# Second normalisation of a two-layer graph network: fp16 halves transposed and multiplied with halves of the score weights, eight tiles in the block ahead, the gap between the layers reordered

## What is computed

```python
# layer 0
h = maximum(layernorm(x), 0)
A = (adj != 0); deg = A.sum(axis=0)
x = x + (A @ (h @ W0 + b0)) / deg[:, None]
# layer 1: attention with 4 heads
h = maximum(layernorm(x), 0)
ht = (h @ W1) split into 4 heads of 512
src, dst = ht @ a_src, ht @ a_dst              # one number for each row and head
e = leaky_relu(src[:, None] + dst[None, :], 0.01) + adj
x = x + mean over heads of softmax(e) @ ht
```

## Time and profile before

| | us |
|---|---|
| median of three timed runs (2478.62 to 2480.04) | 2478.82 |
| the profiled execution, its own time | 2480.18 |
| its span, from the first to the last instruction | 2478.1 |
| TensorE busy in the span | 2454.2 |
| the gap, from PE's first step of the last block (L1508) to its first matmul of layer 1 (L824) | 348.99 to 444.82 |

### The profile page before, as it was taken

The page is one execution under the profiler, slowest core; times in us unless marked ns, Lnnn a source line. Parts: engine busy times, 40 slices in busy tenths (PEclk is TensorE's granted clock), DMA queues, the critical chain, the costliest instruction groups (busy, mean ns, idle before and its releaser), DMA issues.

```text
span 2478.1 us, 42814 instructions
## 1 busy us (share of the span) xinstructions
PE 2454.2 (99%) x12358; PEld 1200.9 (48%) x12358; DVE 1873.2 (76%) x2575; ACT 1260.7 (51%) x1886; POOL 47.8 (2%) x44
## 2 busy tenths in 40 slices
PE   7999999999999999999999999999999999999999
PEld 4444446444444444444444444444444444444787
DVE  7788767976688776887768777687766887667776
ACT  5645645744455444554445544455445554444554
POOL 0000000000000000000000000000000000000000
PEclk9999999999999999999999999999999999999999
DMA  4375746100131001310013100131000300001000
GB/s 149 105 267 186 250 153 220 59 4 5 35 89 34 4 4 34 89 35 4 4 34 89 35 4 4 33 90 35 4 4 26 97 34 3 3 13 49 26 1 9
DMA packets 74079, 143.95 MB, mean 58 GB/s; under 512 B 4473, under 2 KB 11899, under 8 KB 72826
## 3 DMA queue, kind: packets, MB, share of 16 engines
q1 hardware_dynamic: 73978, 142.82, 18.1%
HBM read 129.11 MB, written 13.70 MB: 58 GB/s over the span
## 4 chain that ended last, share of the span: by engine, by line
PE 95%; DVE 2%; DMA 1%; issue 1%; ACT 0%; SPq 0%; DVEq 0%; ACTq 0%
PE z_ps L768 71%; PE o_ps L796 11%; PE o_ps L1455 3%; PE z_ps L1455 3%; PE z_ps L1508 2%; PE o_ps L1420 1%; PE c_ps L1420 1%; DMA ring_reg<-adjT_in 1%; PE c_ps L1455 1%; PE c_ps L1487 1%; DVE hl_reg L969 1%; PE o_ps L1405 1%; PE o_ps L1479 0%; DVE w_reg L1004 0%; PE c_ps L782 0%
## 5 line engine op out<-in xcount | busy, mean ns | idle before, releaser
L768 PE MATMUL z_ps<-hl_reg,h_reg 128*128 (+2 forms) x8712 | 1751.8, 364 | 1.3 <-DVE hl_reg L629 1.3
L768 PEld LDWEIGHTS z_ps<-hl_reg,h_reg 128*128 (+1 forms) x8712 | 852.5, 98 | 897.3 <-issue 1.8
L570 ACT ACTIVATE hl_reg<-t_reg (+2 forms) x363 | 360.7, 994 | 723.3 <-DVE t_reg L657 379.6
L629 DVE TENSOR_TENSOR hl_reg<-t_reg,hl_reg (+2 forms) x363 | 416.5, 1147 | 229.5 <-ACT hl_reg L570 227.1
L555 ACT ACTIVATE t_reg<-ring_reg,vv 128x512 f32 (+3 forms) x728 | 526.4, 770 | 66.2 <-DVE ao_reg L644 60.8
L657 DVE SCALAR_TENSOR_TENSOR t_reg<-t_reg,vv,e_reg (+3 forms) x728 | 510.6, 744 | 9.9 <-issue 7.9
L644 DVE TENSOR_TENSOR ao_reg<-ao_reg,t_reg 128x1024 f32<-128x1024 f32 (+1 forms) x336 | 384.0, 1143 | 0.0
L796 PE MATMUL o_ps<-w_reg,z_reg 128*128 128x512 f16 x1248 | 278.2, 379 | 0.9 <-DVE z_reg L673 0.9
L796 PEld LDWEIGHTS o_ps<-w_reg,z_reg 128*128 128x128 f16 x1248 | 119.8, 98 | 140.9 <-DVE z_reg L673 1.2
L673 DVE SCALAR_TENSOR_TENSOR z_reg<-z_ps,z_reg 128x512 f16<-128x512 f32 (+1 forms) x112 | 73.2, 653 | 151.6 <-ACT z_reg L582 151.6
L463 ACT ACTIVATE e_reg<-e_reg (+2 forms) x91 | 90.5, 995 | 152.5 <-DVE e_reg L474 152.5
(11 more groups left out here) (177 smaller groups left out, 1096.8 us busy)
## 6 DMA issues: line engine op xcount, KB each, us to landing
ring_reg<-adjT_in SPq DMA_DIRECT2D x78, 512.0 KB, 4.6
e_reg<-adjT_in SPq DMA_DIRECT2D x78, 512.0 KB, 3.7
ring_reg<-x_in SPq DMA_DIRECT2D x13, 512.0 KB, 4.1
x_dram<-ring_reg SPq DMA_DIRECT2D x13, 512.0 KB, 5.0
ao_reg<-x_dram SPq DMA_DIRECT2D x6, 1024.0 KB, 5.5
out_dram<-ao_reg SPq DMA_DIRECT2D x6, 1024.0 KB, 4.4
ring_reg<-c_dram SPq DMA_DIRECT2D x23, 256.0 KB, 3.4
h_reg<-x_in SPq DMA_DIRECT2D x3, 1536.0 KB, 16.5
```

The source lines that it names most:

```text
L570: nc.scalar.activation(hl_ring[:, g % HL_RING, 0, :, 0:W], t_ring[:, g % T_RING, :, 0:W], ACT.Copy).then_inc(hi_ready, 1)
L629: nc.vector.tensor_tensor(hl_ring[:, g % HL_RING, 1, :, 0:W], t_ring[:, g % T_RING, :, 0:W], hl_ring[:, g % HL_RING, 0, :, 0:W], ALU.subtr ...
L768: mm = nc.tensor.matmul(z_ps[:, k, 0:W], hk[hs], hl_ring[:, r, ps, u, 0:W], start=first and u == 0 and n == 0, stop=last and u == 1 and n ...
```

## The change

In five parts.

1. **Transposes and scores in fp16.** All tiles but the last one transpose their two fp16 halves, eight transposes of 128x128 fp16 instead of four of fp32; ACT copies 128x1024 fp16 out of PSUM instead of 128x512 fp32; the scores take eight matmuls with fp16 weights (the transposed halves) against 16 columns (high and low half of `wa`). A tile's transpose now waits for the DVE subtraction that makes the low half (`st1_split`), and no longer only for the normalised tile. `wa` is scaled and split in layer 0 by a few small DVE instructions; the two halves of the scores are added before their maximum (`sdc`).
2. **Eight tiles in the block ahead.** The sums and statistics of tiles 0 to 7 are made between steps 80 and 90 of layer 0's `awork` (`early1`), with x loaded into the stage (`load_early`), and tiles 0 to 3 are also normalised and split there. Tiles 4 to 7 follow at the gap's start.
3. **Order in the gap.** `LN1_AT` goes from ceil(6 + 5m/3) to ceil(5 + 1.9m), so that the last of these tiles comes after step 51 and not after step 46; `MR_AT` from 24 to 28. On DVE a pair's subtraction stands between the sums of the group after it. The reductions of the maximum stand behind the scalars of groups 2, 3 and 4 instead of 0, 1 and 2.
4. **The last block's halves.** The halves of tiles 20 to 22 go to a buffer of their own (`late_h`) and are copied into `h16` by a DMA when layer 0 is done with that space; the first loop of layer 1 on PE waits for it (`late_in`).
5. **The tail.** The first activation of layer 1 reads the spread row from PSUM and does not wait for its copy; `keep_clock` is 15, 2, 9 and 11 instead of 14, 0, 12 and 14; ACT's first exponentials, and DVE's first steps of layer 1, stand in another order.

```diff
@@ constants
-        LN1_AT = [math.ceil(6 + 5 * m / 3) for m in range(NT - 1)]
+        LN1_AT = [math.ceil(5 + 1.9 * m) for m in range(NT - 1)]
-        MR_AT = 24
+        MR_AT = 28
+        SUM_G = LAST0 + 2
@@ DVE, layer 0 and the gap
+                def early1(n):
+                    if n == 0:
+                        degrees1(0, EARLY)
+                        x1_sums(0, 2)
+                    if n == 1:
+                        x1_sums(2, 4)
+                    if n == 2:
+                        variances1(0)
+                        ln_scalars(dve, *groups1[0], NG0)
+                    if n == 4:
+                        split1(0)
+                        degrees1(EARLY, 2 * EARLY)
+                    if n == 5:
+                        split1(1)
+                    if n == 8:
+                        x1_sums(4, 6)
+                    if n == 9:
+                        x1_sums(6, 8)
+                    if n == 10:
+                        variances1(1)
+                        ln_scalars(dve, *groups1[1], NG0 + 1)
...
+                    early1(g - SUM_G)
+                degrees1(2 * EARLY, NT)
...
                     for i in range(i0, i1, 2):
-                        for k in range(i, min(i + 2, i1)):
-                            x1_tile(k)
-                        for k in range(i, min(i + 2, i1)):
-                            x1_stats(k)
-                    ln_variances(dve, t0, t1, x1_bst, i1, s_mv1, i1)
-                    while split < min(i0 // 2, LATE_SPLIT):
+                        x1_sums(i, min(i + 2, i1))
+                        if split < min(i0 // 2, PAIRS - 1):
+                            split1(split)
+                            split += 1
+                    variances1(c)
+                    while split < min(i0 // 2, PAIRS - 1):
                         split1(split)
                         split += 1
                     ln_scalars(dve, t0, t1, NG0 + c)
-                    if c < len(late_max):
-                        reduce_max(late_max[c], len(early_max) + c, o_ps[:, 2])
+                    if 0 <= c - 2 < len(late_max):
+                        reduce_max(late_max[c - 2], len(early_max) + c - 2, o_ps[:, 2])
@@ DVE, first steps of layer 1
-            for p in range(1, 4):
-                step(0, 0, p, before=(0, 0, p - 1) if p > 1 else None, lone=p == 1)
...
+            step(0, 0, 1, lone=True)
+            subtract_max(dve, 0, E_PRE0 + 2)
+            lo_part(0, 0, 1)
+            step(0, 0, 2, lone=True)
+            accumulate(0, 0, 1)
+            subtract_max(dve, 0, E_PRE0 + 3)
+            step(0, 0, 3)
+            split1_one(1)
@@ ACT, layer 0 and the gap
                 for g in range(NA):
+                    if g == SUM_G + 2:
+                        ln_sqrt(act, *groups1[0], NG0)
+                    if g == NA - 1:
+                        ln_sqrt(act, *groups1[1], NG0 + 1)
                     degrees(g)
+                    for j in range(2):
+                        if g == SUM_G + 3 + j:
+                            act.wait_ge(s_ln, NG0 + 1)
+                            relu1(2 * j)
+                            relu1(2 * j + 1)
+                            high1(j)
...
+                    if i < NT - 1:
+                        nc.scalar.activation(ht1_16[:, i % 2], o16[:, i % 2].rearrange("p (s k i) -> p s k i", s=2, k=KT),
+                                             ACT.Copy).then_inc(tr_sb, 1)
...
+                for c in range(2, 5):
+                    relus1(c)
+                    for j in (2 * c, 2 * c + 1):
+                        relu1(2 * j)
+                        transposed1(back)
+                        relu1(2 * j + 1)
+                        high1(j)
+                        if j == 2 * c + 1:
+                            next_sqrt(c)
+                        transposed1(back + 1)
+                        back += 2
...
-                for p in range(E_PRE0 - 1):
-                    exp_e(act, 0, p)
+                exp_e(act, 0, 0)
@@ PE
                 def transpose1(i):
-                    pe.wait_ge(st1_ready, i + 1)
...
+                    if i < NT - 1:
+                        pe.wait_ge(st1_split, unit(i) + 1)
+                        pe.wait_ge(s_i16, 1)
+                        h = late_h[:, t - L0] if L0 <= t < L0 + 3 else h16[:, t]
+                        for s in range(2):
+                            for k in range(KT):
+                                mm = nc.tensor.transpose(o16[:, i % 2, (s * KT + k) * P:(s * KT + k + 1) * P],
+                                                         h[:, s, k * P:(k + 1) * P], ident16)
...
                 scores(NT - 2)
                 pe.wait_ge(mr_sb, 1)
                 pe.wait_ge(st1_split, 1)
-                keep_clock(14)
+                keep_clock(15)
                 transpose1(NT - 1)
+                keep_clock(2)
                 scores(NT - 1)
-                keep_clock(12)
+                keep_clock(9)
```

More of the change, by code:

```diff
@@ L1286, in w1_high @@
                     act.wait_ge(wr_in[k], 16)
[L1287 removed]
+                    nc.scalar.activation(w16[:, k, :, 0], w_again, ACT.Copy, scale=wsc[:, 0:1]).then_inc(w_hi, 1)
                 def w0_high(k):
@@ new lines, in high1_one, with relus1, next_sqrt @@
+                    h = late_h[:, 2] if u == 0 else h16[:, tiles1[NT - 1]]
+                    nc.scalar.activation(h[:, 0], ln1_stage[:, (PAIRS - 1) % 2, u], ACT.Copy).then_inc(hi1_done, 1)
+                def relus1(c):
+                    act.wait_ge(s_ln, NG0 + c + 1)
+                def next_sqrt(c):
+                    ln_sqrt(act, *groups1[c + 1], NG0 + c + 1)
+                relus1(1)
+                relu1(4)
+                relu1(5)
+                high1(2)
+                transposed1(0)
@@ new lines, in _ @@
+                for c in (5, 6):
+                    i0 = tiles_of(c)
+                    relus1(c)
+                    relu1(i0)
+                    transposed1(back)
+                    relu1(i0 + 1)
+                    high1(i0 // 2)
+                    next_sqrt(c)
+                    transposed1(back + 1)
+                    back += 2
+                    if c == 5:
+                        max_rows()
+                transposed1(back)
+                relus1(7)
+                relu1(NT - 2)
@@ L1378, in _ @@
+                high1_one(0)
+                for i in range(back + 1, NT - 1):
+                    transposed1(i)
+                next_sqrt(7)
+                relus1(8)
+                relu1(NT - 1)
                 transposed1(NT - 1)
-                for p in range(E_PRE0 - 1):
-                    exp_e(act, 0, p)
+                exp_e(act, 0, 0)
                 act.wait_ge(s_dn, 1)
-                for q, f in ((0, 1.0), (1, SLOPE)):
-                    nc.scalar.activation(ev4[:, q], dn3, ACT.Exp, scale=f / HS).then_inc(s_vv, 1)
+                for q in range(2):
+                    nc.scalar.activation(ev4[:, q], dn3, ACT.Exp, scale=wacoef[:, q:q + 1]).then_inc(s_vv, 1)
@@ L1384, in _ @@
                 act.wait_ge(s_carg, 1)
-                nc.scalar.activation(cc3, cc3, ACT.Exp, scale=1.0 / HS).then_inc(s_cexp, 1)
-                exp_e(act, 0, E_PRE0 - 1)
-                act.wait_ge(cb_ps, 1)
-                act.wait_ge(x1_out[0], 16 * sum((NA + i) % ADJ_RING == 0 for i in range(PAIRS)))
-                nc.scalar.activation(c_bc[:, 0], o_ps[:, 1], ACT.Copy).then_inc(c0_sb, 1)
+                nc.scalar.activation(cc3, cc3, ACT.Exp, scale=wacoef[:, 0:1]).then_inc(s_cexp, 1)
@@ L1391, in c_rows, with c_first @@
+                exp_e(act, 0, 1)
+                def c_first():
+                    act.wait_ge(x1_out[0], 16 * sum((NA + i) % ADJ_RING == 0 for i in range(PAIRS - EARLY)))
+                    nc.scalar.activation(c_bc[:, 0], o_ps[:, 1], ACT.Copy).then_inc(c0_sb, 1)
                 def c_rows():
```

341 lines of the change are left out of this document (215 added, 126 removed).

## The result

| | before | after |
|---|---|---|
| median, us | 2479.33 (2476.95 to 2481.26, 20 runs) | 2482.74 (2480.03 to 2485.62, 20 runs) |
| ratio, 95% interval | | 1.0016 [1.001, 1.0022] |
| the profiled execution, its own time | 2480.18 | 2481.89 |
| its span | 2478.1 | 2480.2 |

The change made the kernel 3.4 us slower by the medians, 0.14 to 0.16%, so within the 0.2% that the prediction called no change (the interval reaches 0.22%). The two profiled executions are 1.7 us apart, their spans 2.1.

A forecast was written before the change was run, and what follows sets the result against it. PE was taken as the bound, busy 99% of the span. Last step 431.9 against 429.7, less 1.0 for the tail, gave +1.2 us on 2480.18, or 2480.0 against the median; range 2470 to 2487.

The forecast's parts named there:

- The tail: From layer 0's last step to layer 1's pairs on PE: -0.6 to -1.2 us, taken as -1.0.
- Both rivals on a slow PE: Gap: fp16 transposes (about 2485 us) or score weights (about 2486) at fp32 pace; 0.25 for either or more low clock.
- the rival with a copy of 0.48: ACT in the gap: copy takes 0.48 us, last step 423.7, or 426.9 with low clock, 2475 us; faster case's chance 0.28.
- the walk: Gap: PE, ACT and DVE queues stepped in order, instructions starting when engine and inputs are ready; last step 427.9 at full clock.
- first maximum: Gap's start: PE's step 4 waits 0.6 us for ACT's copies, standing behind group 1's square root.
- second maximum: Gap: PE waits 3.3 us, from 361.4, for DVE's reduction behind group 2's scalars.
- third maximum: Gap: PE waits 5.8 us, from 372.3, for DVE's reduction behind group 3's scalars.
- waits for copies up to the last step: PE waits for ACT copies behind square roots: 2.1 us at tile 10's scores, 0.3 at 15, 2.2 at 16, 1.8 at 18.
- low clock: PE at 1.2 GHz after long waits in the gap: moves the last step from 427.9 to 431.9 us.
- the sum of work and waits: Gap to the last step: PE's work ending at 411.8 us plus 16.1 of waits gives 427.9 at full clock.
- the ring: Block ahead, steps 80 to 90: it covers PE, so most of DVE's 19.7 us of waits is free for early work.
- PE alone: Gap: PE's work without waits, 62.8 us to step 51, would end at 411.8, 17.9 us earlier.

The follow-up runs named there:

- the experiment on the loads: Changed kernel with the two early loads of x (tiles 0 to 3) issued at step 80 of the adjacency's loads instead of 76: 2480.9 us, ratio 1.0009.
- the tail alone: Kernel before the change plus only its fifth part, without the extra fillers (9 and 11 instead of 12 and 14): 2478.48 us, ratio 0.9996.

## Why the prediction was right, and where a term was wrong

**PE's work fell as forecast.** Transposes 0.445 us a tile (0.44 said), scores 0.20 (0.25 said). The Trainium skill (TensorE: Matmul & The Clock Gate, "LDWEIGHTS (loading the stationary operand)") would have, by its formula, an estimated 107 ns for each of the scores' weight loads; the runs show 25 ns for load and matmul together, here and with the scores doubled. The same page ("Back-to-back issue gap") puts a sustained stream of loads and 128-column matmuls at about 81 ns each; the transposes are such a stream and run at 56. Both rivals on a slow PE fell with these rows.

**The copy on ACT** takes 0.91 us (0.96 said): elements count, not bytes. So the rival with a copy of 0.48 fell; the half-width copy shows that such a copy would be worth 4.6 us with the reductions repaired.

**The waits came where the walk put them.**

| | said | measured |
|---|---|---|
| first sums in the gap, us | 353.1 | 354.5 |
| first maximum, PE's wait | 0.6 (step 4) | 0.4 |
| second maximum | 3.3 | 2.97 |
| third maximum | 5.8 | 5.73 |
| waits for copies up to the last step | 2.1 + 0.3 + 2.2 + 1.8 = 6.4 | 1.92 + 2.01 + 1.59 = 5.5 |
| all waits up to the last step | 16.1 | 14.7 |
| low clock: said, what it adds net of later waits; measured, its own loss | +4.0 | +4.1 |
| the block, start to last step's end, against before | 82.9 - 80.7 = +2.2 | 82.1 - 80.7 = +1.4 |

That the waits for the maxima were the cause, and not only present, is shown twice (from DVE's side and from PE's): without them the kernel is 8 us faster than before. The clock's 4.1 is from that experiment, and close to what the windows give. That it matches the 4.0 said is in part luck. The prediction reckoned with five waits long enough for the low clock and settled near what its walk gave for four such stretches (431.6); for two it had 430.5, so +2.6. Two came: behind 2.97 and 5.73 us, and not behind 1.92, 2.01 and 1.59. But the second was twice as long (5.4 us at 0.50, 2.7 lost), and the measured 4.1 stands beside waits that are already 1.4 shorter than said. The 0.8 by which the block is shorter than said are the scores (23 tiles at 0.05, so 1.2) and the waits (1.4), less about 1.7 in short gaps of PE that the sum of work and waits doesn't hold; it missed 0.7 of such in the kernel before.

**What failed is this step:** "The loads and stores added to SP's queue are 512 KB each, 4.1 us to landing, and go out at least 6 us ahead of use, while DVE is throttled by the ring; I cost them at nothing." The loads were not late for their own use. They made the adjacency late, in a stretch (281 to 307 us) in which the ring doesn't throttle DVE and DVE has no idle time that could take it up. The term is 1.3 us at PE's restart and 1.6 at layer 1, by the experiment on the loads; the first sums in the gap moved with it (353.2 there, 354.5 in the changed kernel, 353.1 said). I had read the ring's cover at steps 80 to 90 in the earlier trace rows and applied it to loads that are issued four steps and more ahead of these.

**The tail** was said to give 1.0 and gives 0.86. These are its rows in the changed kernel:

```profile
434.36 3.40 PE L1730 MATMUL o_ps<-h_reg 128*128 128x512 f16 x15
437.60 0.60 PE L1664 MATMUL o_ps<-ident,z_reg 128*128 128x128 f32 x4
...
442.89 0.65 PE L1743 MATMUL o_ps<-ident,rows_c 128*128 128x128 f32 x4 [1.00 <-ACT rows_c L1557]
...
446.76 5.35 PE L853 MATMUL z_ps<-hl_reg,h_reg 128*128 128x512 f16 x24 [0.74 <-DVE hl_reg L764]
452.63 5.35 PE L797 MATMUL z_ps<-hl_reg,h_reg 128*128 x24 [0.52 <-DVE hl_reg L656]
458.74 3.62 PE L797 MATMUL z_ps<-hl_reg,h_reg 128*128 x16 [0.76 <-DVE hl_reg L656]
```

From the last step to the last tile's transposes 437.60 - 432.6 = 5.0 us against 4.2 (+0.8; +0.85 said). From there to the spread 5.29 against 6.53 in the earlier trace rows and the row that follows them at 440.43 (-1.24; -0.4 to -1.05 said). To the first pair 3.87 against 4.39 (-0.52; -0.6 said). From the first to the third pair 11.98 against 11.88 (+0.1; -0.4 said): the second pair's gain of 0.8 is given back whole at the third, as the tail alone showed too. Two misses of opposite sign.

**The sum.** +1.5 at the block's start, gap +1.4, tail -0.86: +2.0, and the spans differ by 2.1. Of the 1.5 the experiment gives 1.3 to the loads (the block starts at 349.17 there, at 348.99 before); 0.2 has no run of its own. The prediction's +1.2 was +2.2 - 1.0. Its miss is this 1.5 us, against 0.8 too much for the gap: the close total owes something to errors of opposite sign. By the medians the difference is 3.4; what the other 1.3 are is not shown: a profiled execution is one of many, and these spread over 5.6 us. The wait at 305 us, which varies from 1.0 to 2.7 us and once had the low clock behind it, may be a part: with the loads later, ten runs spread over only 1.3 us.

**What stays open.** No run undid the fp16 transposes alone or the eight early tiles alone, so their shares are worked out and not measured. Moving the subtraction back was not tried without other edits either. Nor was `late_h` tried by itself; PE's first loop of layer 1 shows no wait for it.

## What to carry to other kernels

When the bound engine's work is cut, walk its queue and its partners' in order with the durations of the trace before counting the gain: here PE alone would have ended 17.9 us earlier than before, and 14.7 us of waits plus 4.1 of low clock behind them took it all, and three short reductions set one place too late in another queue were more than half of it. An instruction that another engine waits for belongs right behind the point where its input is there, ahead of any instruction that itself waits. A load that is early enough for its own use can still cost time, if it is issued ahead of transfers that another engine is about to need and has no idle time to wait for. Look at that engine's idle time in the stretch in which the load goes out, not in the one in which it is used; the share of the DMA engines didn't tell, since they were full behind the loads in the place that cost time and in the one that didn't.

## What the runs showed of the hardware

- In the gap and at 305 us the low clock follows some waits of about 2 us and not others. Behind 1.97 us it fell in the kernel before; behind 1.92 and 2.01 in the changed kernel, behind 2.14 with the reductions moved and behind 2.01 at 305 us with the square root moved, the granted clock stayed at 1.00. Behind 2.74, 2.97 and 5.73 us it fell. So a gap of PE near 2 us has an uncertain price of about 1.6 us. Nor is one long wait needed: in the tail of the kernel before, the granted clock is 0.60 over 436.16 to 440.43, and the waits ahead of it are 0.39 and 0.69 us; the tail alone repeats it, while the changed kernel's tail, with waits of 0.26 and 1.00, stays at 1.00.
- A matmul of fp16 with 16 columns and its own weight load takes 0.025 us in a row of eight or sixteen, about as the earlier trace rows has it with one column. At this size the count of instructions sets the time, and not whether there is one column or 16.
- 1 MB of loads put in a stretch at 0.86 of the DMA engines' time made DVE wait 1.33 us more, and PE 1.4 us where it had waited 0.2; from profile to profile PE's wait there is 1.0 to 2.7 us with these loads and 0.2 to 0.6 without them or with them later.
